# Biases of six of eight expert units written into the bank by ScalarE, in a fused decoder layer

## The reference, cut to what matters

```python
x = _layernorm(x + self_attention(x))
x = _layernorm(x + cross_attention(ctx, ctx, x) @ Wo.T + bo)
weights = softmax(x @ gate_w)              # 8 experts, top 2 taken
e0 = silu(x @ w0.T + b0)
e1 = silu(x @ w1.T + b1)
x = _layernorm(x + e0 * fw0 * m0 + e1 * fw1 * m1)
```

## Time and profile before

| | |
|---|---|
| median of 3 runs | 1772.83 us (1769.48 to 1775.35) |
| span of the profiled execution | 1773.4 us |
| PE busy | 1681.7 us, 95% |
| DVE busy | 1254.6 us, 71% |
| POOL busy | 1161.8 us, 66% |
| ACT busy | 974.2 us, 55% |
| DMA queue q1 | 48.2% of 16 engines' span |

### The profile page before, as it was taken

How to read it: one execution, slowest core, us unless ns; L and a number is a source line. 1 busy time by engine, 2 the same in 40 slices (tenths; PEclk the granted TensorE clock), 3 DMA queues, 4 the chain that set the end, 5 groups by cost and what they waited for, 6 DMA issues and landing times.

```text
span 1773.4 us, 30895 instructions
## 1 busy us (share of the span) xinstructions
PE 1681.7 (95%) x10626; PEld 1111.0 (63%) x10626; DVE 1254.6 (71%) x2785; ACT 974.2 (55%) x1939; POOL 1161.8 (66%) x964
## 2 busy tenths in 40 slices
PE   5999999999999989999998999999999999999998
PEld 4766666666666547877863556566565656656566
DVE  5677777777777666767876776877778686777745
ACT  4555555555555443433445565656666665666554
POOL 2556556556555554744565977878788786878874
PEclk9999999999999989999998999999999999999999
DMA  6556555555555464576625543535344354534210
GB/s 199 147 149 168 145 152 156 153 156 165 141 153 153 122 194 152 181 219 185 193 66 155 144 115 88 139 90 155 91 114 114 82 138 99 144 93 108 63 42 31
DMA packets 167273, 237.29 MB, mean 134 GB/s; under 512 B 22087, under 2 KB 73287, under 8 KB 167117
## 3 DMA queue, kind: packets, MB, share of 16 engines
q1 hardware_dynamic: 167116, 235.31, 48.2%
HBM read 91.57 MB, written 41.94 MB: 75 GB/s over the span
## 4 chain that ended last, share of the span: by engine, by line
PE 68%; DVE 12%; POOL 8%; DMA 4%; issue 4%; ACT 2%; SPq 1%; POOLq 0%; DVEq 0%; ACTq 0%
PE bank L1652 9%; POOL cross_added L1974 7%; PE bank L201 5%; PE bank L202 5%; PE bank L203 5%; DVE bank L585 5%; PE bank L1522 5%; PE bank L1490 5%; PE bank L1461 5%; PE bank L369 4%; PE bank L305 4%; PE bank L356 3%; DVE bank L548 2%; PE bank L1558 2%; PE bank L329 2%
## 5 line engine op out<-in xcount | busy, mean ns | idle before, releaser
L1471 DVE TENSOR_REDUCE cross_negmax<-bank 128x1 f32<-128x512 f32 x512 | 338.7, 674 | 149.8 <-PE bank L1461 147.2
L1738 ACT ACTIVATE cpt<-bank 128x512 f32<-128x512 f32 x512 | 297.7, 595 | 143.6 <-PE bank L1490 140.1
L548 DVE CUSTOM_DVE_ANT_0 bank<-bank,future 128x128 f32<-128x128 f32 (+3 forms) x512 | 243.0, 488 | 177.8 <-PE bank L356 177.7
L430 ACT ACTIVATE pt<-bank 128x256 f32<-128x256 f32 (+3 forms) x512 | 217.5, 444 | 260.2 <-PE bank L305 256.1
L1974 POOL TENSOR_TENSOR cross_added<-cross_added,cpt 128x2048 f32<-128x2048 f32 x61 | 280.0, 4591 | 11.5 <-ACT cpt L1738 11.0
L618 POOL TENSOR_SCALAR_AFFINE_SELECT pt<-pt 128x512 f32<-128x512 f32 x128 | 81.1, 634 | 246.8 <-ACT pt L430 246.8
L1490 PE MATMUL bank<-cqk 98*128 98x512 f32 x512 | 227.4, 444 | 7.1 <-ACT cpt L1738 6.2
L1461 PE MATMUL bank<-cqk 96*128 96x512 f32 x512 | 212.5, 418 | 10.7 <-DVE cross_negmax L1471 8.6
L1974 POOL TENSOR_TENSOR cross_added<-cpt,cpt 128x2048 f32<-128x2048 f32 x32 | 146.6, 4581 | 84.0 <-ACT cpt L1738 84.0
L305 PE MATMUL bank<-qk 98*128 98x256 f32 (+2 forms) x512 | 180.6, 359 | 8.4 <-ACT pt L430 3.9
L356 PE MATMUL bank<-qk 96*128 96x256 f32 (+2 forms) x512 | 169.5, 335 | 4.4 <-DMA qk<-stage 4.4
(11 more groups left out here) (207 smaller groups left out, 3623.8 us busy)
## 6 DMA issues: line engine op xcount, KB each, us to landing
qk<-stage SPq DMA_DIRECT2D x384, 128.0 KB, 2.3
cqk<-cstage SPq DMA_DIRECT2D x384, 128.0 KB, 2.3
scratch_memory<-memory SPq DMA_DIRECT2D x32, 512.0 KB, 3.8
ma<-scratch_memory SPq DMA_DIRECT2D x32, 512.0 KB, 3.9
raw<-in_x_t SPq DMA_DIRECT2D x32, 256.0 KB, 2.9
v<-in_x SPq DMA_DIRECT2D x32, 256.0 KB, 3.2
scratch_y_ar<-y_ar SPq DMA_DIRECT2D x32, 256.0 KB, 2.4
my_ar<-scratch_y_ar SPq DMA_DIRECT2D x32, 256.0 KB, 4.6
```

The lines of the kernel that those rows point to most:

```text
L548: dve.tensor_tensor_reduce(out=scores, in0=scores, in1=sh.future[:, SEQ - P * (qt + 1):SEQ], scale=-1.0, scalar=-NEG, op0=ALU.add, op1=ALU ...
L1471: dve.reduce_max(s.negmax[gm % 2][:, col:col + 1], max_bank(sh, m)[:, :], AX, negate=True).then_inc(s.dve_max, 1)
L1738: act.activation(s.pt[step % 3][:, j, :], sh.bank[2 + n % 2][:, :], ACT.Exp, scale=SCALE_CROSS).then_inc(s.act_exp, 1)
```

## The change

Units 2 to 7 of each batch but the last no longer start with a bias product. In the slot before the unit's first, ScalarE writes the bias into the bank with an ACTIVATE Copy, and the twelve products are added onto it. Units 0 and 1, the projections and the tail keep a bias product. Bias rows `b0` and `b1` are loaded for this onto all 128 partitions; there is no free stretch of 2 KB for the second, so it stands in two halves, and odd units take two ACTIVATEs. The second half lies where `future`, the mask of the self-attention, stood.

The three bias rows of the remaining products now stand in one tile of 128 x 512: rows 0 to 2 the high parts, rows 32 to 34 the rests. A tile `pick` of 3 x 128 columns, made of the identity, chooses the row.

```diff
-        self.rows = sb("bias_rows", [P, 3, DIM], F32R)
-        self.row_ones = sb("bias_ones", [P, P], F32R)
+        self.rows, self.pick = sb("bias_rows", [P, DIM], F32R), sb("bias_pick", [P, 3, P], F32R)
+        self.bias0, self.bias1 = sb("bias_0", [P, DIM]), sb("bias_1", [P, DIM // 2])
...
-    dve.wait_ge(cw.small_landed, 16 * 7)
+    dve.wait_ge(cw.small_landed, 16 * 10)
...
-    dve.tensor_copy(cw.rows[:, :, :], s.rows_raw[:, :, :]).then_inc(cw.dve_small, 1)
+    dve.tensor_copy(cw.rows[:, :], s.rows_raw[:, :]).then_inc(cw.dve_small, 1)
     dve.wait_ge(cw.dve_small, 3)
-    dve.tensor_tensor(cw.rows[32:33, :, :], s.rows_raw[32:33, :, :], cw.rows[32:33, :, :].bitcast(F32),
+    dve.tensor_tensor(cw.rows[32:35, :], s.rows_raw[32:35, :], cw.rows[32:35, :].bitcast(F32),
                       ALU.subtract).then_inc(cw.dve_small, 1)
+    dve.tensor_tensor(cw.pick[:, :, :], sh.ident[:, 0:3].unsqueeze(2).to_broadcast([P, 3, P]),
+                      sh.ident[:, 32:35].unsqueeze(2).to_broadcast([P, 3, P]), ALU.add).then_inc(cw.dve_small, 1)
...
-        pool.memset(cw.row_ones[:, :].bitcast(F32), 1.0).then_inc(cw.pool_zero, 1)
...
-            pool.memset(s.rows_raw[:, :, :], 0.0).then_inc(cw.pool_zero, 1)
+            pool.memset(s.rows_raw[:, :], 0.0).then_inc(cw.pool_zero, 1)
...
     if i == SMALL + 1:
         memory_load_bias(sp, s, cw, 2)
+        sp.dma_start(cw.bias0[:, :], t["b0"].partition_broadcast(P)).then_inc(cw.small_landed, 16)
+        for half, tile in enumerate((cw.bias1, sh.bias_end)):
+            src = t["b1"][half * (DIM // 2):(half + 1) * (DIM // 2)].partition_broadcast(P)
+            sp.dma_start(tile[:, :], src).then_inc(cw.small_landed, 16)
...
-    pe.matmul(bank[:, :], cw.row_ones[:, :], cw.rows[:, i, :], start=True, stop=False)
+    pe.matmul(bank[:, :], cw.pick[:, i, :], cw.rows[:, :], start=True, stop=False)
...
         else:
-            pe.wait_ge(s.dve_u, UNITS * b + u - 1)
-        cross_bias(pe, cw, bank, 1 + i)
+            pe.wait_ge(s.act_bias, bias_written(b, u))
+        if u < 2:
+            cross_bias(pe, cw, bank, 1 + i)
...
+    u, r = divmod(slot - EXPERT + 1, UNIT_SLOTS)
+    if r == 0 and 2 <= u < UNITS:
+        cross_bias_written(act, s, cw, sh, b, u)
...
+def cross_bias_written(act, s, cw, sh, b, u):
+
+    bank = sh.bank[6 + u % 2]
+    act.wait_ge(s.dve_u, UNITS * b + u - 1)
+    if u % 2 == 0:
+        act.activation(bank[:, :], cw.bias0[:, :], ACT.Copy).then_inc(s.act_bias, 1)
+    else:
+        act.activation(bank[:, 0:DIM // 2], cw.bias1[:, :], ACT.Copy).then_inc(s.act_bias, 1)
+        act.activation(bank[:, DIM // 2:], sh.bias_end[:, :], ACT.Copy).then_inc(s.act_bias, 1)
```

More of the change, by code:

```diff
@@ L90, in __init__ @@
         self.ident = sb("ident", [P, P])
+        late = sb.at
         self.future = sb("future", [P, SEQ], BF16)
+        self.bias_end = Place(nc, late, sb.at)("bias_1_end", [P, DIM // 2])
         self.ones = sb("ones", [P, HEAD_DIM])
@@ L781, in __init__ @@
         self.y_hi, self.y_lo = [even[0], odd[0]], [even[1], odd[1]]
-        self.rows_raw = Place(nc, ATTENTION + 2 * STACK_BYTES, TOP)("bias_raw", [P, 3, DIM])
+        self.rows_raw = Place(nc, ATTENTION + 2 * STACK_BYTES, TOP)("bias_raw", [P, DIM])
         self.fold_landed, self.raw_landed = sem("fold_landed"), [sem(f"mraw_landed{i}") for i in range(2)]
@@ L1098, in memory_round_vector @@
     if i == SMALL + 3:
-        memory_small_weights(dve, s, cw)
+        memory_small_weights(dve, s, cw, sh)
     t = i - BEHIND
@@ L1113, in memory_folded, with memory_small_weights @@
     act.activation(cw.wo[:, c, :], sh.bank[6][:, :], ACT.Copy).then_inc(cw.act_fold, 1)
-def memory_small_weights(dve, s, cw):
-    dve.wait_ge(cw.small_landed, 16 * 7)
+def memory_small_weights(dve, s, cw, sh):
+    dve.wait_ge(cw.small_landed, 16 * 10)
     dve.tensor_copy(cw.gate_hi[:, :, :], cw.gate_raw[:, :, :]).then_inc(cw.dve_small, 1)
@@ L1219, in memory_load_bias @@
 def memory_load_bias(sp, s, cw, i):
-    for row in (0, 32):
+    for row in (i, 32 + i):
         src = s.t[("bo", "b0", "b1")[i]].partition_broadcast(1)
-        sp.dma_start(s.rows_raw[row:row + 1, i, :], src).then_inc(cw.small_landed, 16)
+        sp.dma_start(s.rows_raw[row:row + 1, :], src).then_inc(cw.small_landed, 16)
 def memory_sync(sp, s, third, cw, sh):
@@ L1249, in memory_round_sync @@
     if i == SMALL:
-        sp.wait_ge(cw.pool_zero, 3)
+        sp.wait_ge(cw.pool_zero, 2)
         memory_load_bias(sp, s, cw, 0)
@@ L1363, in __init__ @@
         self.pool_k, self.pool_add, self.pool_ones = sem("pool_ck"), sem("pool_cross_add"), sem("pool_cqk_ones")
-        self.dve_norm = sem("dve_cross_norm")
+        self.dve_norm, self.act_bias = sem("dve_cross_norm"), sem("act_bias")
         self.pe_po, self.pe_x2t, self.pe_gate, self.pe_lt = sem("pe_po"), sem("pe_x2t"), sem("pe_gate"), sem("pe_logits")
@@ L1586, in cross_batch @@
                     pe.wait_ge(second.dve_s, NG)
-                    pe.wait_ge(cw.dve_small, 4)
+                    pe.wait_ge(cw.dve_small, 5)
             else:
@@ L1590, in cross_batch @@
             if b == 0:
-                pe.wait_ge(cw.pool_zero, 3 + GROUPS)
+                pe.wait_ge(cw.pool_zero, 2 + GROUPS)
             cross_bias(pe, cw, bank, 0)
@@ L1651, in cross_expert @@
         w = s.e_lo if which == 2 else s.e_hi
-        done = pe.matmul(bank[:, :], x[:, c, tile_of(k)], w[:, i, c, :], start=False, stop=(part == 11))
+        done = pe.matmul(bank[:, :], x[:, c, tile_of(k)], w[:, i, c, :], start=False, stop=(part == 11),
+                         skip_group_check=(u >= 2))
     if third == UNIT_SLOTS - 1 and half == 1:
@@ L1724, in cross_slot_scalar @@
     for b, slot in behind(n):
-        cross_batch_scalar(act, s, sh, b, slot)
+        cross_batch_scalar(act, s, cw, sh, b, slot)
     if 0 <= n < NS:
@@ L1739, in cross_slot_scalar, with cross_batch_scalar @@
                        scale=SCALE_CROSS).then_inc(s.act_exp, 1)
-def cross_batch_scalar(act, s, sh, b, slot):
+def cross_batch_scalar(act, s, cw, sh, b, slot):
     if slot in APPLY:
@@ L1774, in cross_batch_scalar, with bias_written @@
         s.ln3.apply(act, b, k, s.x2[:, k, :], s.x2[:, k, :])
+def bias_written(b, u):
+    return 9 * b + 3 * (u // 2 - 1) + (1, 3)[u % 2]
+def cross_bias_written(act, s, cw, sh, b, u):
[6 more added lines that the diff above has]
+        act.activation(bank[:, DIM // 2:], sh.bias_end[:, :], ACT.Copy).then_inc(s.act_bias, 1)
 def gate_scratch(bank, i, tiles=TILES):
@@ L1909, in cross_constants @@
 def cross_constants(pool, s, cw):
-    pool.wait_ge(cw.dve_small, 4)
+    pool.wait_ge(cw.dve_small, 5)
     ones_rows(pool, s.kq, s.pool_ones)
```

## The result

| | after | before, beside it | ratio after / before, 95% interval |
|---|---|---|---|
| first measurement | 1758.24 us (4 runs, 1757.73 to 1765.41) | 1773.24 us (4 runs) | 0.9929 [0.9912, 0.9946] |
| five more rounds | 1760.29 us (6 runs) | 1772.41 us (23 runs) | 0.9939 [0.9918, 0.9960] |

The change makes the kernel 0.6 to 0.7% faster; 1763.1 us was predicted. The first median lies 0.3 us under the lower edge of the predicted range (1758.5), the second inside it.

What follows compares the result with a forecast made beforehand. PE's issue was taken as the bound, with ScalarE having 39 us a batch free. -9.8 + 0.3 + 0.85 - 1.0 = -9.65 us gave 1763.1 us, 0.55% faster, range 1758.5 to 1768.8.

Steps and rivals of the forecast that it cites:

- Part 1: Cross stage, PE: 42 of 96 bias products go at 0.233 us each, 9.8 us gained, 1.40 us a batch.
- Part 2: Cross stage, ScalarE's bias writes: 0.6 us each, 0.5 us lost per unit; PE's waits for them cost 0.3 us in sum.
- The wait of 0.3 us in all: PE waiting for unit 4's bias write: 0.05 us taken in each of six batches, priced at 0 to 0.2.
- the silu moves up by that of unit 2, 0.23: Before unit 4: silu 0.23 us earlier, PE's first product 0.70, leaving the write a margin of 0.27 us.
- the forecast of over 0.5 us: Expert units other than unit 4: the bias write would end with over 0.5 us left before PE's product.
- Part 3: POOL's additions move up only 1.0 us against PE's 1.4; PE waits in the next batch's first group, 0.85 us lost.
- PE now waiting for POOL in the first group: Expected sign in the profile: PE waits for POOL's third addition in the first group of the batches.
- Part 4: Memory stage, round 8: VectorE's bias-row preparation falls from 2.70 to 1.68 us, gaining 1.0 us (bounds 0.4 and 1.14).
- Much comes back: Rival: POOL moves up 0.3 us a batch, PE waits 1.0 in six batches, 1768.3 us; 0.22 together with half value.
- Half value: Rival: a removed product gives PE half of 0.233 us, 1767 us; chance 0.22 together with the case that much comes back.
- More than forecast: Rival: PE's later waits shrink, POOL's adds fall better, the round's wait goes whole: 13 us gained, 1759.9 us; chance 0.11.
- Slower: Rival: each unit waits for its bias write, at 0.6 us each +14 us, 1787 us; chance 0.05.

## Why the prediction was right, step by step

**Part 1** was right in mechanism and size. With the products back a batch is 103.84 to 103.87 us, without them 102.43 to 102.70, and the difference falls on the six slots in which units start, 0.24 us each. The distance between two starts, 0.233 us, was the price, and not the duration of 0.40 us. The Trainium skill, "TensorE: Matmul & The Clock Gate", section "Back-to-back issue gap", has 0.131 us for a sustained stream, which this trace doesn't bear out. The page's 0.216 us for an isolated one would have been close.

**Part 2**, the write's duration (0.60 us) and its overlap (0.53 us from its start to the weighing's) were as forecast. The wait of 0.3 us in all didn't come. The step that failed is "the silu moves up by that of unit 2, 0.23". Against the earlier trace rows, PE's product is 10.40 us earlier in the profile after, the silu 10.17, so the silu lost 0.23 and not 0.47 on the product: it moved up by two of the three products. In the kernel before, this is VectorE in front of that silu, and PE:

```profile
1388.42 0.69 DVE L1471 TENSOR_REDUCE cross_negmax<-bank 128x1 f32<-128x512 f32 x1 [0.84 <-PE bank L1461]
1389.02 0.95 DVE L1809 RECIPROCAL bank<-bank 128x128 f32<-128x128 f32 x1
```

```profile
1387.28 0.40 PE L1572 MATMUL bank<-bias_rows,bias_ones 128*128 128x512 f32 x1
...
1387.98 0.40 PE L1461 MATMUL bank<-cqk 96*128 96x512 f32 x1
```

The silu doesn't stand behind PE's unit 2 alone. On VectorE it is queued behind a reduce that waits for a maximum's score, and PE issues that score behind unit 3's bias product (1387.28), which went too. The row of the silu shows no idle time before it; the releaser has to be looked for two instructions further up. Between the write's end and the product lay 0.51 us, where the forecast had 0.27, and the weight load in front took 0.24 of it. What unit 4 had free was 0.46 us by the product's start and 0.37 by its slot (each write twice), not 0.07.

For the other units the forecast of over 0.5 us holds as the change stands: at units 2, 5 and 6 the write ends 0.81, 1.21 and 0.95 us before the product, and at units 3 and 7 over 3 us before. At unit 6 it doesn't hold once ScalarE falls behind, as with each write twice.

**Part 3** had the place right and the size wrong: forecast 0.85 us given back, measured 0. The exponential before unit 4 comes 0.04 us later against the batch's slots, not 0.27 (0.23 is again unit 3's product). The two gaps behind it closed whole, so POOL moved up by some 1.2 to 1.3 us instead of 1.0. PE's sum starts 0.18 to 0.26 us behind the addition's end in the six groups concerned (0.26 in the one shown above), where 0.146 would be a wait; so it is short of one by as little as 0.04 us. In the second profile of the kernel after, the distances are 0.15 to 0.33 us, and where it is 0.146 the sum comes no later in the batch than elsewhere. "PE now waiting for POOL in the first group" did not happen at any cost that can be seen. That the mechanism is real shows with each write twice, where PE waits there and loses 0.17 to 0.21 us; that it costs nothing in the change as it stands is a matter of hundredths, and partly luck.

**Part 4**: the three durations were forecast as 0.43, 0.69 and 0.56 us and measured as 0.42, 0.68 and 0.56. Lateness fell from 1.94 to 0.83, a little more than forecast, and the round gave 1.1 us instead of 1.0. The longer casts confirm the cause. The three new loads cost nothing: VectorE's small weights start right behind the instruction before, with no wait.

**Sum.** The two terms that were to give back are zero and the round is worth 0.1 more: 9.65 + 0.3 + 0.85 + 0.1 = 10.9 us. A batch came out at 102.43 to 102.61 us, at and just under the forecast of 102.5 to 102.8. This is the ratio of the second measurement, 0.9939, and inside the interval of the first, 0.9929. That the first median lies another 2 us lower is, as far as the profiles show, transfers that fall differently; that the change itself moves them was not excluded, and the 0.6 to 1.0 us of group 28 stays open. The kernel without any bias has the same 0.9940, which speaks for 10.9 as what the change is worth.

**Rivals.** "Much comes back" is refuted: nothing does. "Half value" too: each product gave 0.24. "More than forecast" named the round's whole wait (1.14) and no loss, which is what came, though its 2 us more of other waits are not shown. "Slower" needs the write to come late, and one slot later it did: 2.2 us lost a batch against 1.4 gained.

## What to carry to other kernels

Price what leaves an engine that is never idle by the distance between starts, and give it back only where a wait follows; here all of it stayed. When you work out by how much a releaser moves up, go back through the queue of its own engine to the last instruction with an idle time: the one just before it may hide the true releaser. Work that moves to an engine with idle time is free only if it stands early enough in that engine's order: the same change, with its 63 writes one slot ahead, made the kernel 0.6% faster, and with them one slot later 0.2% slower than before.

## What the hardware showed that was not expected

A tile of 3 x 512 and one of 1 x 512 x 3 hold the same numbers, but VectorE's subtraction took 0.68 us on three partitions and 1.75 us on one: here the columns counted, and not the partitions. ScalarE's copy into a bank (0.60 us for 512 columns) takes as long as its exponential out of one (0.595 us), and two writes of 256 columns in a row start 0.32 us apart, so that the odd units' split costs 0.69 us from first start to last end against 0.60.
